# A fused embedding, attention and expert kernel: the split of the negated maxima moves to GpSimd, and the embedding steps run two at a time

## The chip, the core and the metric

The kernel runs on one core of one Trainium2 chip. The metric is the time of one execution on the device in microseconds, the median of three runs. The core has TensorE (PE, with PEld for its weight loads), VectorE (DVE), ScalarE (ACT), GpSimd (POOL) and SyncE (SP), which here only issues transfers. Each engine runs its own instructions in program order, and waits on semaphores for the others.

## What is computed

Eight batches of 1024 image tokens and 32 text tokens (1056 in all) with 64 features. The reference, cut to its body:

```python
h = _L0_tok_ref(x, L0_tok_W)                       # patches, real FFT, one linear map: (8, 1024, 64)
h = jnp.concatenate([h, txt], axis=1)              # (8, 1056, 64)
h = h + attn(_layernorm(h))                        # 4 heads of 16, softmax over all 1056 tokens, projection + bias
h = h + ffn(_layernorm(h))                         # top 2 of 8 experts, exact gelu, hidden width 128
```

The softmax of row n is exp(s - m) / sum exp(s - m), with m the largest score of the row. Everything is float32 in and out.

## The kernel before

**Two phases.** Phase 1 is attention for the eight batches, one *pass* each (passes 0 to 7), phase 2 the experts for four pairs of batches. Attention needs queries and keys to f32 precision, but multiplies in bf16: each value is split into three bf16 parts, and 96 rows of `q_stack` and `k_stack` hold the products of parts that matter. Three more rows of `q_stack` hold the negated row maximum, itself in three bf16 parts, against rows of ones in `k_stack`. So the score matmul delivers s - m, and ScalarE only takes the exponential.

**A pass and its units.** The queries stand in three chunks (384, 384 and 288 columns). A pass has 99 *units*, 33 per chunk: unit 0 of a chunk scores the 32 text keys, the other 32 score one tile of 128 keys for one head (L1185), and ScalarE exponentiates each (L927). The probabilities meet the values eight units later, four heads at a time in f32 (L1163), into one PSUM bank that ScalarE empties into `heads_out` (L912) six units into the next chunk. Scores rotate over three banks.

**Side work between the units.** Every engine runs the same generator, `run_phase1`. At each unit it does, in this order: `attend_unit`, `max_steps`, `weigh_unit` (L1163), `side_steps`. The tables `AT_...` give the unit of each side step:

- *Maxima.* For the next batch, 70 fills of PSUM per pass (25, 25 and 20 for the three chunks) recompute the scores without maximum (L1222, L1228, L1233), and VectorE reduces each (L1035, L1038, L1043). After the last of a chunk VectorE combines them into `negm` (L1049, and L1054 for the text queries), splits this in four small dependent steps into `neg_part` (L1058, L1060, L1063, L1065), and TensorE transposes that with an identity (the *shift*, L1244, L1248). VectorE copies the result to `m_part` (L1074) and SP sends it into `q_stack` with three DMAs (L790). The score of the chunk's first unit waits for these.
- *Where they stand.* `MAX_PLACE` spreads the 73 entries of `MAX_ORDER` over the units. The shift of a chunk follows two maxima of the next one: chunk 0 at unit 90 of the pass before its own, chunk 1 at unit 26, chunk 2 at unit 52 of the pass before. The last maximum of chunk 0 is at unit 85, of chunk 1 at 22, of chunk 2 at 48, and the first of the next batch at 49. Entries rotate over three banks by their index modulo 3; index 72 and the next index 0 share a bank. The very last shift stands at `LAST_SHIFT`, unit 49 of the last pass.
- *Tokenising* (passes 0, 2 and 4, for the pair of batches after next). Two halves of the image tokens are each built from eight embedding steps. A step is two f32 matmuls of 512 columns side by side in the two column halves of the array (L1199), in the trace four records, as f32 takes two passes. They stand at units 34, 36, ..., 48 and 50, 52, ..., 64, all in one side bank. ScalarE copies the first half to `h_new`, VectorE the second; norm, statistics and its square roots follow at 66 to 90.
- *Projecting* queries and keys at 36, 39, 42 (odd passes) or 92, 94, 97 (even): here GpSimd makes the third bf16 part (L856).
- *Finishing* the previous pass: reciprocals of the denominators on VectorE, their spread by DMA, the normalisation of the heads on GpSimd at units 24, 26, 28 (L862), and the output projection on TensorE at 27, 30, 33 (L1300), added to `h_res` by VectorE (L1104). Passes 1 to 7 have this.

In phase 1 GpSimd has nothing but L856 and L862. TensorE runs ahead of ScalarE by at most three units.

Of the kernel before, what the change touches and what calls it, by code (L numbers as in the profile page):

```python
# [8 lines left out]
ALU = mybir.AluOpType  # L9
# [16 lines left out]
NCH = 3  # L26
# [32 lines left out]
AT_FINISH = [27, 30, 33]  # L59
AT_SPREAD = [0, 2, 2]  # L60
AT_STACK = [1, 3]
AT_EMBED = [list(range(34, 49, 2)), list(range(50, 65, 2))]
AT_VARY = [74, 75, 76]
AT_ROOT = [77, 78, 79, 80]
AT_TOKENISE = [AT_EMBED[0][-1], AT_EMBED[1][-1], 66, 68, 70, 72, AT_VARY[-1], 86, 88, 90]
# [5 lines left out]
AT_LOAD = {"first": [2 + 3 * k for k in range(X_DMAS - X_EARLY)], "load": [30 + 3 * k for k in range(X_DMAS)]}  # L71
AT_FFN = 60

def max_order():

    order = [(0, 0, 0), (0, 0, 1), (-1, NCH - 1, None)] + [(0, 0, i) for i in range(2, MAX_OF[0])]
    for c in range(1, NCH):
        order += [(0, c, 0), (0, c, 1), (0, c - 1, None)] + [(0, c, i) for i in range(2, MAX_OF[c])]
    return order

# [44 lines left out]
def build(nc, x, txt, tok_w, w_qkv, w_proj, b_proj, gate_w, gate_b, w1, b1, w2, b2, consts, out):  # L126
    with ExitStack() as ctx:
# [3 lines left out]
        def sem(name):  # L131
            return ctx.enter_context(nc.semaphore(name))
# [77 lines left out]
        max_scores = sem("max_scores")  # L210
        max_done = sem("max_done")
        neg_max = sem("neg_max")
        neg_step = sem("neg_step")
        shifted = sem("shifted")
        scores_ready = sem("scores_ready")
# [81 lines left out]
        def side_steps(u, stages, b, par, q, g):  # L297

            ahead = q + 1 if par else q + 2
            order = []  # L300
            for i in range(3):
                if "finish" in stages and u == AT_SPREAD[i]:
                    order.append(("spread", i, b - 1, 1 - par, q, g))
            for i in range(2):
                if "following" in stages and u == AT_STACK[i] + (AT_FIRST["project"][-1] if "first" in stages else 0):
                    order.append(("stack", i, b + 1, 1 - par, q + 1, g))
            if u == AT_RECIP and "finish" in stages:
                order.append(("recip", 0, b - 1, 1 - par, q, g))
            if "load" in stages and u in AT_LOAD["load"]:
                order.append(("load", AT_LOAD["load"].index(u), None, None, q + 2, g))  # L310
            if "first" in stages and u in AT_LOAD["first"]:
                order.append(("load", X_EARLY + AT_LOAD["first"].index(u), None, None, 1, g))
            if "first" in stages and u == AT_FFN:
                order.append(("ffn", 0, None, None, None, g))
            for name, stage, at, t, tpar, pair in (
                    ("first", "project", AT_FIRST["project"], b + 1, 1 - par, q + 1),
                    ("first", "values", AT_FIRST["values"], b + 1, 1 - par, q + 1),
                    ("values", "values", AT_VALUES, b + 1, 1 - par, q + 1),
                    ("finish", "finish", AT_FINISH, b - 1, 1 - par, q),
                    ("tokenise", "tokenise", AT_TOKENISE, None, None, q + 2),  # L320
                    ("project", "project", AT_PROJECT["odd" if par else "even"], b + 2, par, ahead)):
                if name in stages:
                    if stage == "finish" and u in AT_NORMALISE:
                        order.append(("normalise", AT_NORMALISE.index(u), t, tpar, pair, g))
                    if stage == "tokenise" and u in AT_VARY[:-1]:
                        order.append(("vary", AT_VARY.index(u), None, None, pair, g))
                    if u in at:
                        order.append((stage, at.index(u), t, tpar, pair, g))
                    if stage == "tokenise":
                        for i in range(2):  # L330
                            if u in AT_EMBED[i][:-1]:
                                order.append(("embed", (i, AT_EMBED[i].index(u)), None, None, pair, g))
                        if u in AT_ROOT:
                            order.append(("root", 1 + AT_ROOT.index(u), None, None, pair, g))
                    g = g + USES[stage]
            return order
# [96 lines left out]
        def max_slot(t, c, i, n):  # L433

            if isinstance(t, int) and t == B - 1 and (c, i) == (NCH - 1, None):
                return MAXU * B - 1, 0, MAXU * B - 1
            t, n = (t + 1, n - MAXU) if n >= MAXU else (t, n)
            at = MAXU * t + n - 1
            if isinstance(t, int) and t == 0:
                at = n if n < 2 else n - 1  # L440
                return at, n % 3, at - 1 if n in (3, 4) else at - 2
            return at, n % 3, at if n == 0 else at - 2

        ROOT_STEPS = 16
# [291 lines left out]
        with nc.Block() as block:  # L736
# [112 lines left out]
            @block.gpsimd  # L849
            def _(pool):  # L850
                def side(stage, i, t, par, pair, g):
                    if stage == "project":

                        pool.wait_ge(part2_done, NCH * t + i + 1)
                        at_least(pool, stacked, 16 * 12 * t)
                        nc.gpsimd.tensor_tensor(qk_part[2][:, chunk[i]], qk_rest[:, chunk[i]], qk_part[1][:, chunk[i]],  # L856
                                                ALU.subtract).then_inc(part3_done, 1)
                    elif stage == "normalise":

                        pool.wait_ge(recip_spread, 16 * H * (t + 1))  # L860
                        pool.wait_ge(side_free, g)
                        nc.gpsimd.tensor_tensor(on[:, chunk[i]], ot[par][:, chunk[i]], recip[:, chunk[i]], ALU.mult)\  # L862
                          .then_inc(on_ready, 1)

                run_phase1(nc.gpsimd, lambda b, par, u, g: None, side, lambda b, par: None)

                def product(p, c, e):

                    n = PER_PAIR * p + E * c + e
                    dst = acc[p % 2][:, chunk[c]]  # L870
                    if (c, e) == (0, 0):
                        at_least(pool, out_full, FOLDS * (p - 1))
                    pool.wait_ge(y_read, n + 1)
                    if e > 0:
                        pool.wait_ge(summed, n)
                    nc.gpsimd.tensor_tensor(dst, h2_all[:, p, chunk[c]] if e == 0 else dst, prod[:, n % N_PROD, :],  # L876
                                            ALU.add).then_inc(summed, 1)

                run_phase2(nc.gpsimd, product, lambda eng, name, i, p: None, lambda p, i: None, side)

# [112 lines left out]
            def _(dve):  # L994
# [25 lines left out]
                def side(stage, i, t, par, pair, g):  # L1020
# [4 lines left out]
                    elif stage == "maxima":  # L1025
# [18 lines left out]
                              .then_inc(max_done, 1)  # L1044
                        if i == MAX_OF[c] - 1:
                            dve.wait_ge(max_done, at + 1)
                            step = 4 * (NCH * t + c)
                            kinds = slice(0, 1) if c < NCH - 1 else slice(1, 3)
                            last = nc.vector.tensor_reduce(negm[:, kinds.start, 0:nt, :], parts[:, 0:nt, :, :], AX.X,  # L1049
                                                           ALU.max, negate=True)  # L1050
                            if c == NCH - 1:
                                for h in range(H):
                                    rows = slice(32 * h, 32 * h + 32)
                                    last = nc.vector.tensor_reduce(negm[rows, 2, nt, h:h + 1], max_tail[rows, :],  # L1054
                                                                   AX.X, ALU.max, negate=True)
                            last.then_inc(neg_step, 1)
                            dve.wait_ge(neg_step, step + 1)
                            nc.vector.tensor_copy(neg_part[:, kinds, :, 0, :], negm[:, kinds, :, :]).then_inc(neg_step, 1)  # L1058
                            dve.wait_ge(neg_step, step + 2)
                            nc.vector.tensor_tensor(neg_rest[:, kinds, :, :], negm[:, kinds, :, :],  # L1060
                                                    neg_part[:, kinds, :, 0, :], ALU.subtract).then_inc(neg_step, 1)
                            dve.wait_ge(neg_step, step + 3)
                            nc.vector.tensor_copy(neg_part[:, kinds, :, 1, :], neg_rest[:, kinds, :, :]).then_inc(neg_step, 1)  # L1063
                            dve.wait_ge(neg_step, step + 4)
                            nc.vector.tensor_tensor(neg_part[:, kinds, :, 2, :], neg_rest[:, kinds, :, :],  # L1065
                                                    neg_part[:, kinds, :, 1, :], ALU.subtract).then_inc(neg_max, 1)
                    elif stage == "shift":

                        c = i[0]
# [335 lines left out]
```

## Time and profile before

| | |
|---|---|
| median of 3 runs | 876.16 us (873.74, 876.16, 883.76) |
| profiled execution | 872.1 us, its span 870.3 us |
| mean granted TensorE clock in it | 0.944 of full speed |
| prologue, to the first scores | to 89 us |
| attention, eight passes | 89 to about 683 us |
| experts | to the end |

The time of an execution includes a little beyond the span that the profile covers. In the rows, a line of a timeline has the start in us from the span's start, the length in us, the engine, the line of the kernel and what is written from what; in square brackets the engine's idle time just before and what ended it. Matmul records overlap: their lengths include a tail that the next one hides, so distances from start to start tell what an instruction costs. "POOLq" and the like are an engine's queue.

### The profile page before, as it was taken

How to read it: one execution, taken by the hardware profiler on the slowest of the kernel's cores; microseconds unless marked ns; L12 is line 12 of the kernel's file. 1: busy time of each engine (PE TensorE's matmuls, PEld its weight loads, DVE VectorE, ACT ScalarE, POOL GpSimd, SP SyncE). 2: the span in 40 equal slices, each digit the busy share in tenths (PEclk: the TensorE clock that was granted, in tenths of full speed). 3: DMA queues.
4: the chain of work that ended last, by engine and by line, in shares of the span. 5: the costliest groups of instructions: out<-in, count | busy, mean ns of one | idle time of the engine just before them, and what ended most of it. 6: DMA issues, size and time to landing. Idle time of an engine off the chain costs nothing.

```text
span 870.3 us, 14564 instructions
## 1 busy us (share of the span) xinstructions
PE 799.5 (92%) x5448; PEld 314.4 (36%) x5448; DVE 551.8 (63%) x1193; ACT 462.2 (53%) x1061; POOL 131.7 (15%) x148
## 2 busy tenths in 40 slices
PE   1958999999999989999999999999989899999995
PEld 1341322443332244333224433433334444545442
DVE  6038564678876467887656788788864075655632
ACT  1110454566664456666445666667655655464662
POOL 0010100012000001200000120010100055363664
PEclk9955699999999999999998999999988999999998
DMA  9329301016621001662100110220000736555571
GB/s 190 74 69 175 89 25 38 1 61 127 111 77 65 1 2 59 129 110 73 69 2 1 47 45 1 60 83 1 16 2 1 137 82 121 108 120 110 109 145 25
DMA packets 61934, 60.05 MB, mean 69 GB/s; under 512 B 23840, under 2 KB 54056, under 8 KB 61864
## 3 DMA queue, kind: packets, MB, share of 16 engines
q1 hardware_dynamic: 59264, 57.58, 30.2%
q10 hardware_dynamic: 2599, 1.54, 0.9%
q8 instruction: 43, 0.70, 0.3%
q14 instruction: 28, 0.22, 0.1%
HBM read 38.88 MB, written 2.57 MB: 48 GB/s over the span
## 4 chain that ended last, share of the span: by engine, by line
PE 78%; DVE 11%; ACT 4%; issue 2%; DMA 2%; POOL 0%; ACTq 0%; SPq 0%; POOLq 0%
PE bank L1163 15%; PE bank L1185 14%; PE bank L1222 11%; PE bank L1199 7%; PE bank L1331 7%; PE bank L1314 7%; DVE max_parts L1035 4%; PE bank L1276 3%; PE bank L1168 2%; PE bank L1300 2%; ACT probs L927 2%; PE bank L457 2%; PE bank L508 2%; PE bank L1280 1%; PE bank L633 1%
## 5 line engine op out<-in xcount | busy, mean ns | idle before, releaser
L1035 DVE TENSOR_REDUCE max_parts<-bank 128x1 f32<-128x512 f32 x512 | 331.3, 685 | 128.5 <-PE bank L1222 126.2
L927 ACT ACTIVATE probs<-bank 128x384 f32<-128x384 f32 (+1 forms) x768 | 311.6, 465 | 183.3 <-PE bank L1185 182.2
L1185 PE MATMUL bank<-q_stack,k_stack 99*128 99x384 bf16 (+1 forms) x768 | 227.6, 324 | 5.4 <-ACT probs L927 5.0
L1222 PE MATMUL bank<-k_stack,q_stack 96*128 96x512 bf16 x512 | 204.5, 402 | 6.3 <-DMA k_stack<-part 3.4
L1163 PE MATMUL bank<-probs,v_tiles 128*32 128x384 f32 (+1 forms) x1536 | 157.3, 482 | 2.2 <-ACT heads_out L912 2.1
L1185 PEld LDWEIGHTS bank<-q_stack,k_stack 99*128 99x128 bf16 x768 | 72.8, 100 | 199.9 <-ACT probs L927 151.7
L975 ACT ACTIVATE hid<-bank,biases 128x704 f32<-128x704 f32 x96 | 77.7, 844 | 58.9 <-PE bank L1331 58.6
L1123 DVE SCALAR_TENSOR_TENSOR prod<-bank,biases,cwb 128x352 f32<-128x352 f32 x96 | 55.3, 579 | 66.3 <-PE bank L1314 59.0
L876 POOL TENSOR_TENSOR acc<-acc,prod 128x352 f32<-128x352 f32 x84 | 78.2, 931 | 62.1 <-DVE prod L1123 58.1
L856 POOL TENSOR_TENSOR part<-qk_rest,part 128x352 bf16<-128x352 f32 x24 | 20.4, 851 | 365.8 <-DVE part L1083 365.8
L1314 PE MATMUL bank<-hid,w_sb 128*64 128x352 f32 x384 | 68.5, 476 | 1.5 <-DVE prod L1123 1.5
L1199 PE MATMUL bank<-x,tok_m 128*64 128x512 f32 x256 | 67.9, 628 | 1.7 <-DVE tok_m L1017 1.1
L1222 PEld LDWEIGHTS bank<-k_stack,q_stack 96*128 96x128 bf16 x512 | 50.6, 99 | 50.5 <-DVE max_parts L1035 24.2
L862 POOL TENSOR_TENSOR on<-heads_out,recip 128x352 f32<-128x352 f32 x24 | 21.9, 936 | 223.1 <-DMA recip<-recip_rows 223.1
L1163 PEld LDWEIGHTS bank<-probs,v_tiles 128*32 128x32 f32 x1536 | 30.7, 109 | 62.9 <-ACT probs L927 43.2
L1331 PE MATMUL bank<-xn,w_sb 64*128 64x352 f32 x192 | 36.4, 498 | 0.6 <-ACT hid L975 0.6
L1331 PE MATMUL bank<-xn_odd,w_sb 64*128 64x352 f32 x192 | 35.9, 491 | 0.6 <-ACT hid L975 0.6
L1314 PEld LDWEIGHTS bank<-hid,w_sb 128*64 128x64 f32 x384 | 23.5, 138 | 35.2 <-issue 28.3
L920 ACT ACTIVATE probs_tail<-bank 128x384 f32<-128x384 f32 (+1 forms) x24 | 11.1, 463 | 35.6 <-PE bank L1181 35.6
L936 ACT ACTIVATE part<-bank 128x352 bf16<-128x352 f32 x24 | 11.1, 464 | 30.5 <-PE bank L1276 30.4
L508 PE MATMUL bank<-ident_half,root_part 128*64 128x128 bf16 (+1 forms) x432 | 17.7, 228 | 8.5 <-DVE root_part L498 6.2
L1276 PE MATMUL bank<-xn,qkT 64*128 64x352 f32 x48 | 23.9, 592 | 1.2 <-DVE qk_rest L1080 0.6
(146 smaller groups left out, 579.2 us busy)
## 6 DMA issues: line engine op xcount, KB each, us to landing
cwb<-gates_by_expert SPq DMA_DIRECT2D x24, 704.0 KB, 11.3
x<-in_x SPq DMA_DIRECT2D x48, 256.0 KB, 7.0
q_stack<-part SPq DMA_DIRECT2D x48, 132.0 KB, 2.5
k_stack<-part SPq DMA_DIRECT2D x42, 132.0 KB, 2.4
x<-in_x SPq DMA_DIRECT2D x4, 576.0 KB, 12.0
h_res<-h_new SPq DMA_DIRECT2D x4, 528.0 KB, 3.0
recip<-recip_rows SPq DMA_DIRECT2D x32, 66.0 KB, 2.5
h_all<-h_res SPq DMA_DIRECT2D x4, 528.0 KB, 4.0
```

The costliest lines, as they stand in the source:

```text
L876: nc.gpsimd.tensor_tensor(dst, h2_all[:, p, chunk[c]] if e == 0 else dst, prod[:, n % N_PROD, :], ALU.add).then_inc(summed, 1)
L927: nc.scalar.activation(probs[:, group % 3, h, 0:n], src, ACT.Exp, scale=SCALE).then_inc(exp_done, 1)
L975: nc.scalar.activation(hid[:, n % N_HID, :, :], psum[:, first:first + 2, 0:CH], ACT.Gelu, bias=b1_sb[:, e:e + 1]).then_inc(gelu_done, 1)
L1035: nc.vector.tensor_reduce(max_parts[:, c, H * j + h, i % 2:i % 2 + 1], src[:, :], AX.X, ALU.max)\
L1123: nc.vector.scalar_tensor_tensor(out=prod[:, n % N_PROD, :], in0=banks[4 + n % 2][:, 0:CH], scalar=b2_sb[:, e:e + 1], in1=cwb[p % 2][:, e, ...
L1163: last = nc.tensor.matmul(o_bank[32 * h:32 * h + 32, 0:n], v_tiles[par][:, kt, h, :], probs[:, group % 3, h, 0:n], start=(kt == 0), stop=F ...
L1185: last = nc.tensor.matmul(bank[:, 0:n], ks[par][0:ROWS + 3, h, P * kt:P * kt + P], qs[par][0:ROWS + 3, h, QC[qc]], start=True, stop=True)
L1199: last = nc.tensor.matmul(bank[D * bp:D * bp + D, :], tok_m[:, part, :], xt[bp][:, first:first + NPATCH // 2, t4, :], start=(part == 0), s ...
L1222: last = nc.tensor.matmul(bank[:, :], queries(h, j), ks[par][0:ROWS, h, HALF * (i % 2):HALF * (i % 2) + HALF], start=True, stop=True)
L1276: last = nc.tensor.matmul(bank[:, 0:CH], qkT[rows, :], xn[rows, chunk[i]], start=True, stop=True)
L1314: last = nc.tensor.matmul(banks[4 + n % 2][D * bp:D * bp + D, 0:CH], w2_sb[:, m % E, :], hid[:, n % N_HID, bp, :], start=True, stop=True)
L1331: last = nc.tensor.matmul(banks[2 * (n % 2) + bp][:, 0:CH], w1_sb[rows, e, :], xn2[p % 2][rows, chunk[c]], start=True, stop=True)
```

## The change

- The four splitting steps leave VectorE and are issued by GpSimd, at the unit of the chunk's last maximum. VectorE signals a new semaphore, `neg_found`, after the reductions; GpSimd waits for it, and for its own previous step before each further one, and signals `neg_max` at the end.
- The shift stands behind three maxima of the next chunk instead of two: chunk 0 at unit 92, chunk 1 at 27, chunk 2 at 53; the third maximum takes its former place. `max_slot` is adapted. The last shift stays at 49.
- The embedding steps stand two at a time at units 34, 38, 42, 46 and 50, 54, 58, 62; the ones that end a half, and so the copies into `h_new`, at 46 and 62. Within a unit they come ahead of the other tokenising steps.

```diff
-AT_EMBED = [list(range(34, 49, 2)), list(range(50, 65, 2))]
+AT_EMBED = [[34, 34, 38, 38, 42, 42, 46, 46], [50, 50, 54, 54, 58, 58, 62, 62]]
...
+SHIFT_AFTER = 3
 def max_order():
-    order = [(0, 0, 0), (0, 0, 1), (-1, NCH - 1, None)] + [(0, 0, i) for i in range(2, MAX_OF[0])]
+    order = [(0, 0, i) for i in range(SHIFT_AFTER)] + [(-1, NCH - 1, None)] + [(0, 0, i) for i in range(SHIFT_AFTER, MAX_OF[0])]
     for c in range(1, NCH):
-        order += [(0, c, 0), (0, c, 1), (0, c - 1, None)] + [(0, c, i) for i in range(2, MAX_OF[c])]
+        order += [(0, c, i) for i in range(SHIFT_AFTER)] + [(0, c - 1, None)] + [(0, c, i) for i in range(SHIFT_AFTER, MAX_OF[c])]
...
+                    if stage == "tokenise":
+                        for i in range(2):
+                            for part, at_part in enumerate(AT_EMBED[i][:-1]):
+                                if u == at_part:
+                                    order.append(("embed", (i, part), None, None, pair, g))
...
-                at = n if n < 2 else n - 1
-                return at, n % 3, at - 1 if n in (3, 4) else at - 2
+                at = n if n < SHIFT_AFTER else n - 1
+                return at, n % 3, at - 1 if n in (SHIFT_AFTER + 1, SHIFT_AFTER + 2) else at - 2
...
# GpSimd, side():
+                    elif stage == "maxima" and i[1] == MAX_OF[i[0]] - 1:
+                        c = i[0]
+                        k = NCH * t + c
+                        kinds = slice(0, 1) if c < NCH - 1 else slice(1, 3)
+                        pool.wait_ge(neg_found, k + 1)
+                        nc.gpsimd.tensor_copy(neg_part[:, kinds, :, 0, :], negm[:, kinds, :, :]).then_inc(neg_step, 1)
+                        pool.wait_ge(neg_step, 3 * k + 1)
+                        nc.gpsimd.tensor_tensor(neg_rest[:, kinds, :, :], negm[:, kinds, :, :],
+                                                neg_part[:, kinds, :, 0, :], ALU.subtract).then_inc(neg_step, 1)
+                        pool.wait_ge(neg_step, 3 * k + 2)
+                        nc.gpsimd.tensor_copy(neg_part[:, kinds, :, 1, :], neg_rest[:, kinds, :, :]).then_inc(neg_step, 1)
+                        pool.wait_ge(neg_step, 3 * k + 3)
+                        nc.gpsimd.tensor_tensor(neg_part[:, kinds, :, 2, :], neg_rest[:, kinds, :, :],
+                                                neg_part[:, kinds, :, 1, :], ALU.subtract).then_inc(neg_max, 1)
...
# VectorE, side("maxima"), after the reductions:
-                            last.then_inc(neg_step, 1)
-                            dve.wait_ge(neg_step, step + 1)
...
+                            last.then_inc(neg_found, 1)
```

## Rows read from the trace of the kernel before

**Rows 1.** The page: TensorE's busy time; the last chain by engine.

```profile
PE 799.5 (92%) x5448; PEld 314.4 (36%) x5448; DVE 551.8 (63%) x1193; ACT 462.2 (53%) x1061; POOL 131.7 (15%) x148
...
PE 78%; DVE 11%; ACT 4%; issue 2%; DMA 2%; POOL 0%; ACTq 0%; SPq 0%; POOLq 0%
```

**Rows 2.** Two stretches: busy us of each engine, granted clock, DMA.

```profile
220.00:290.00 70.00, 68.64 (x486) 23.35 (x482) 50.49 (x100) 42.14 (x109) 2.72 (x3) 1.00 0.32 78
...
430.00:500.00 70.00, 68.51 (x478) 24.98 (x476) 43.00 (x97) 37.38 (x95) 2.56 (x3) 0.95 0.05 15
```

**Rows 3.** Timeline of TensorE, units 38 to 40: start us, length us.

```profile
276.02 0.38 PE L1222 MATMUL bank<-k_stack,q_stack 96*128 96x512 bf16 x1
276.33 1.08 PE L1199 MATMUL bank<-x,tok_m 128*64 128x512 f32 x4
277.34 0.34 PE L1185 MATMUL bank<-q_stack,k_stack 99*128 99x384 bf16 x1
277.52 0.38 PE L1222 MATMUL bank<-k_stack,q_stack 96*128 96x512 bf16 x1
277.74 0.33 PE L1185 MATMUL bank<-q_stack,k_stack 99*128 99x384 bf16 x1
277.99 1.08 PE L1199 MATMUL bank<-x,tok_m 128*64 128x512 f32 x4
```

**Rows 4.** Timeline of TensorE in the prologue: 28 embedding records in a row.

```profile
29.08 6.17 PE L1199 MATMUL bank<-x,tok_m 128*64 128x512 f32 x28
```

**Rows 5.** Timeline, shift of chunk 1, pass 1: VectorE, TensorE, GpSimd.

```profile
198.46 0.19 DVE L1049 TENSOR_REDUCE negm<-max_parts 128x12 f32<-128x36 f32 x1
...
199.29 0.17 DVE L1065 TENSOR_TENSOR neg_part<-neg_rest,neg_part 128x12 bf16<-128x12 f32 x1
...
199.61 0.23 PE L1244 MATMUL bank<-ident_half,neg_part 128*36 128x128 bf16 x1
199.77 0.34 PE L1185 MATMUL bank<-q_stack,k_stack 99*128 99x384 bf16 x1
...
200.44 0.81 PE L1300 MATMUL bank<-on,projT 128*64 128x352 f32 x2
...
196.01 2.70 POOL L862 TENSOR_TENSOR on<-heads_out,recip 128x352 f32<-128x352 f32 x3 [12.68 <-DMA recip<-recip_rows]
```

**Rows 6.** Timelines: dependent additions; start after VectorE; stretched subtraction.

```profile
857.02 4.14 POOL L876 TENSOR_TENSOR acc<-acc,prod 128x352 f32<-128x352 f32 x4 [0.72 <-DVE prod L1123]
...
216.06 0.34 DVE L1083 CAST part<-qk_rest 128x352 bf16<-128x352 f32 x1
...
216.48 0.85 POOL L856 TENSOR_TENSOR part<-qk_rest,part 128x352 bf16<-128x352 f32 x1 [1.29 <-DVE part L1083]
...
351.19 0.62 DVE L1060 TENSOR_TENSOR neg_rest<-negm,neg_part 128x12 f32<-128x12 f32 x1
```

**Rows 7.** Timeline of TensorE at the shift of chunk 0 in pass 1.

```profile
241.03 0.22 PE L1244 MATMUL bank<-ident_half,neg_part 128*36 128x128 bf16 x1 [0.16 <-DVE neg_part L1065]
```

**Rows 8.** Timeline of TensorE at units 48 and 49: passes 1, then 2.

```profile
218.29 0.34 PE L1185 MATMUL bank<-q_stack,k_stack 99*128 99x384 bf16 x1
219.08 0.38 PE L1222 MATMUL bank<-k_stack,q_stack 96*128 96x512 bf16 x1 [0.45 <-DVE max_tail L1043]
...
287.27 1.08 PE L1199 MATMUL bank<-x,tok_m 128*64 128x512 f32 x4
```

**Rows 9.** Timeline of TensorE at unit 41 of pass 6.

```profile
580.71 0.38 PE L1222 MATMUL bank<-k_stack,q_stack 96*128 96x512 bf16 x1
581.38 0.53 PE L1163 MATMUL bank<-probs,v_tiles 128*32 128x384 f32 x4 [0.29 <-ACT heads_out L912]
```

**Rows 10.** Timeline at the last shift: VectorE, then TensorE.

```profile
646.56 0.62 DVE L1054 TENSOR_REDUCE negm<-max_tail 32x1 f32<-32x3 f32 x4
...
648.18 0.26 PE L1244 MATMUL bank<-ident_half,neg_part 128*36 128x128 bf16 x1 [2.06 <-DVE neg_part L1065]
```

**Rows 11.** Timeline of TensorE at the first shift, in the prologue.

```profile
84.18 0.26 PE L1244 MATMUL bank<-ident_half,neg_part 128*36 128x128 bf16 x1 [0.98 <-DVE neg_part L1065]
```

More of the change, by code:

```diff
@@ L212, in build @@
         neg_max = sem("neg_max")
+        neg_found = sem("neg_found")
         neg_step = sem("neg_step")
@@ L329, in side_steps @@
                     if stage == "tokenise":
-                        for i in range(2):
-                            if u in AT_EMBED[i][:-1]:
-                                order.append(("embed", (i, AT_EMBED[i].index(u)), None, None, pair, g))
                         if u in AT_ROOT:
@@ L1046, in side @@
                             dve.wait_ge(max_done, at + 1)
-                            step = 4 * (NCH * t + c)
                             kinds = slice(0, 1) if c < NCH - 1 else slice(1, 3)
@@ L1055, in side @@
                                                                    AX.X, ALU.max, negate=True)
-                            last.then_inc(neg_step, 1)
-                            dve.wait_ge(neg_step, step + 1)
[L1058 to L1066, printed above, removed]
+                            last.then_inc(neg_found, 1)
                     elif stage == "shift":
```

## The prediction

> **What bounds the kernel now.** I read the page first. TensorE is busy 92% of the span and holds 78% of the chain that ended last, VectorE 11% and GpSimd nothing [rows 1]. The windows by stage come next: in attention TensorE is busy 68.5 of 70 us while VectorE has 43 to 51, ScalarE 37 to 42, GpSimd under 3 [rows 2]. So in attention only two things count: what the instructions in TensorE's own queue cost, and how long that queue stands at a wait. Work taken off VectorE is worth nothing unless TensorE waits for it. For both I read the timelines of TensorE unit by unit, comparing the distance from one start to the next for the same pair of lines.
>
> **Embedding steps in pairs.** One step is four records (two column halves at once, two passes). Alone between bf16 matmuls it holds TensorE from 276.33 to 277.34, 1.01 us. Also, a bf16 matmul of 512 columns before it takes 0.31 us to the next start (276.02 to 276.33) where before another bf16 matmul it takes 0.22 (277.52 to 277.74) [rows 3]. Together 1.10 us. In an unbroken run 28 records, seven steps, take 6.17 us; without the tail of the last record (0.6) that is 0.43 per pair of records, 0.86 per step [rows 4]. The rest, 0.24 us, is the price of each change of kind. Of 16 steps per tokenising pass eight no longer pay it. One of those (unit 36) stood right behind the weighted values, also f32, and paid only about 0.14. So 7 x 0.24 + 0.14 = 1.8 us per pass, in passes 0, 2 and 4: **-5.5 us**. The bounds are 0 (the second step of a pair loads weights as slowly as a lone one) and this; I take this, since the run of rows 4 is the same instructions back to back.
>
> **What the lone steps covered.** Moving steps to 34, 38, 42, 46 leaves units 40 and 48 without one. (a) Unit 48 holds the last maximum of chunk 2, unit 49 the first of the next pass, and by the numbering both use bank place 0. In pass 1, without embedding, TensorE goes from the scores at 218.29 to the maximum at 219.08, waiting for VectorE: 0.79 us where 0.17 is usual. In pass 2 the step at 287.27, one microsecond long, stands between and the wait is gone [rows 3, 8]. It comes back in three passes: 3 x 0.62 = **+1.9**. (b) Unit 41 multiplies the first probabilities of chunk 1 into the bank that ScalarE empties (L912) after unit 39. In pass 6, with no side work at 40, that costs 0.67 us after the maximum instead of 0.31 [rows 3, 9]. In tokenising passes the step at unit 40 (277.99) hides it; after the change the pair at 38 ends before the scores of unit 39, which release ScalarE, so it hides nothing: 3 x 0.36 = **+1.1**. The other moves (34, 50, the copies of h_new two units earlier) wait for nothing new: the pair at 34 still follows the same residual addition, and the loads of x are long done.
>
> **The split on GpSimd.** It is 24 chains (3 chunks, 8 passes) of four small dependent operations, two conversions and two subtractions of 12 or 24 elements; VectorE keeps the reductions. On VectorE each takes 0.17 us and the chain ends 0.81 us after the maxima are negated (198.65 to 199.46); TensorE starts the shift 0.15 later [rows 5]. The trace has no small operation on GpSimd. Bounds: VectorE's 0.17 below, and 0.93 above, its own operation over 352 elements [rows 6]. With 12 elements instead of 352 the lower end is nearer; I take 0.20 and call it x. Between dependent operations of GpSimd lie (4.14 - 0.93) / 3 - 0.93 = 0.14 us; from VectorE's end to GpSimd's start 0.08 (216.40 to 216.48) [rows 6]; from GpSimd to TensorE I take VectorE's 0.15. From the negated maxima to the shift: 0.08 + 4x + 3 x 0.14 + 0.15 = 1.45 us, where it was 0.96.
>
> **What queues behind that chain.** GpSimd runs in program order. The chain of chunk 1 stands at unit 22, the normalisations of the previous pass at 24, 26 and 28. Before, all three ran as soon as the reciprocals had landed, 196.01 to 198.71; the output projection at unit 27 (L1300, 200.44) needs the first [rows 5]. Now none can start before the maxima are negated (198.65) and split: 198.65 + 0.08 + 0.80 + 0.42 + 0.93 + 0.15 = 201.03. TensorE stands 0.59 us at L1300, in five of the seven passes with a projection. The shift in front of it, now at unit 27, is due 1.3 to 1.4 us after the negation and waits within that time. In passes 3 and 7 VectorE's own subtraction was stretched by the normalisations beside it (0.62 against 0.17) [rows 6], so the projection was late already: +0.14 and nothing. Together **+3.1**. The later normalisations (0.89 apart) stay ahead of units 30 and 33.
>
> **The other shifts.** Chunk 0, unit 90: TensorE waited about 0.2 us in four passes without tokenising [rows 7]; two units later it is due 1.8 us after the negation, and the wait goes: **-0.8**. Chunk 2 is due at 1.6 us, with 24 elements ready at 1.53: nothing. The last shift of all keeps its place, one unit behind the last maximum, where TensorE waits 2.06 us [rows 10]; the chain ends it: 1.01 us becomes 1.53, **+0.5**. In the prologue TensorE waits for the first split too [rows 11], but VectorE does a third maximum meanwhile (0.6), less than the 0.8 it no longer spends: the copy of m_part comes about 0.1 later there and once more in pass 0, **+0.2**. SP's three DMAs per shift keep their order except that one load of text now goes before those of chunk 0; they land over half a microsecond before the scores.
>
> **Sum.** -5.5 + 1.9 + 1.1 + 3.1 - 0.8 + 0.5 + 0.2 = **+0.5 us** on the profiled 872.1: 872.6. The median of the runs is 876.2, 4.1 higher, so 876.7. TensorE's granted clock, 0.95 in one stretch of pass 4 and 1.00 in another [rows 2], means half speed for some 7 of 70 us; such stretches may move or go with any change, worth up to 3 us. The likeliest case's own range is 873 to 881.
>
> **Rivals.**
> - *GpSimd's small operations are slow* (x = 0.4; slower). Seven projections wait 0.8 more (5.6), four shifts of chunk 0 0.4 each (1.7), four of chunk 2 0.65 (2.6), the last one 0.8, the prologue 1.6: +12.8, 889 by the median. It passes 1% at x = 0.35. For it: nothing small is measured. Against: 12 elements are few. Chance 0.20.
> - *A pair costs what two steps cost.* The 5.5 are missing: +6.0, 882.7. Rows 4 speak against. Chance 0.08.
> - *The waits do not come.* If GpSimd ends before L1300 (the negation comes earlier, x small) and units 41 and 49 find their banks free: -5.5 - 0.8 + 0.7 = -5.6, 870.6. For it: VectorE has less to do. Against: the negation follows the maximum of unit 22, which TensorE times. Chance 0.15.
> - *VectorE's relief carries* (faster). It loses 24 x 0.8 = 19 us, and holds 11% of the chain, 96 us [rows 1]. If a tenth of that goes, -9.5 with the rest at zero, 867. It decides if TensorE's waits for max banks were backlog; the ones I found follow TensorE's own last fill. Chance 0.10.
>
> **Chances.** The forecast has 0.47. One per cent, about what a measurement of this kernel can tell from no change, is 8.8 us. Faster comes from the relief and a little from the third rival with a better clock: 0.12. Slower is the slow GpSimd and part of the second with a worse clock: 0.24. Within 1%: 0.64. The range 868 to 889 leaves out the end of the fourth rival and the worst half of the first.
>
> **What would show it.** Right: eight records of L1199 in a row, 1.87 us to the next start; L1300 of unit 27 waiting for GpSimd's L862 by about 0.6 us; a start-to-start of 0.8 at unit 49 and 0.67 at 41 in tokenising passes; the four GpSimd operations at 0.2 us each. Wrong: those at 0.3 or more, or TensorE's waits for max_parts shrinking all over.

## The result, and the profile after

| | before | after |
|---|---|---|
| median, first measurement (18 executions each) | 880.85 us (869.0 to 891.6) | 867.11 us (860.9 to 871.7) |
| ratio of the two, 95% interval | | 0.990 (0.9875 to 0.993) |
| median, all executions with a granted clock on record (82 and 30) | 875.4 us | 868.4 us |
| mean of the same | 878.5 us | 867.8 us |
| lowest granted clock of an execution | 0.915 | 0.942 |
| profiled execution, its granted clock | 872.1 us, 0.944 | 870.6 us, 0.946 |

The change makes the kernel 1.0% faster in the first measurement and 0.5% in its repeat (e4 below: ratio 0.995, 0.992 to 0.999), and much steadier. The ratio leaves out slow executions, those that lie far above the fastest of their kernel; the medians and means here count all, because the spread turned out to be part of the effect. The first 18 executions of the kernel before (mean 881.3 us) have no granted clock on record and are not among the 82. The two profiled executions differ by 1.5 us only: 872.1 is under the median of before, 870.6 above that of after. Neither stands for its kernel's median, so the profile is read below by passes, and the time by many executions.

The page of the kernel after, its span, TensorE's busy time and the shares of the last chain:

```profile
span 868.8 us, 14564 instructions
...
PE 791.5 (91%) x5448; PEld 318.2 (37%) x5448; DVE 535.8 (62%) x1097; ACT 459.6 (53%) x1061; POOL 151.6 (17%) x244
...
PE 76%; DVE 10%; ACT 5%; issue 3%; DMA 2%; POOL 2%; ACTq 1%; SPq 0%; POOLq 0%
```

The chain is TensorE's as before [rows 1]; GpSimd now has 2% of it. Lengths of the passes, from the first scores of one pass to those of the next (chunk by chunk in brackets), from the timelines of L1181 before and L1190 after, where no clock change falls in:

| pass | before | after |
|---|---|---|
| 1 | 63.6 (22.3, 23.8, 17.6) | 63.7 (22.6, 23.7, 17.4) |
| 2, tokenising | 88.7 (22.3, 38.2, 28.2) | 87.4 (22.6, 37.4, 27.4) |
| 3 | 64.1 (22.7, 23.8, 17.6) | 63.7 (22.6, 23.7, 17.4) |

**GpSimd's small operations**, by the tile they write (count, then shortest, median and longest in ns):

```profile
L869 POOL CAST neg_part<-negm x24: 193/194/205, 82.8 to 645.0; 128x12 bf16<-128x12 f32 x16, 128x24 bf16<-128x24 f32 x8
L871 POOL TENSOR_TENSOR neg_rest<-negm,neg_part x24: 213/214/239, 83.1 to 645.3; 128x12 f32<-128x12 f32 x16, 128x24 f32<-128x24 f32 x8
L874 POOL CAST neg_part<-neg_rest x24: 194/195/204, 83.4 to 645.6; 128x12 bf16<-128x12 f32 x16, 128x24 bf16<-128x24 f32 x8
L876 POOL TENSOR_TENSOR neg_part<-neg_rest,neg_part x24: 213/214/241, 83.6 to 645.9; 128x12 bf16<-128x12 f32 x16, 128x24 bf16<-128x24 f32 x8
```

They take 0.19 and 0.21 us, the 0.20 that the sum was made with. The shift of chunk 1 in pass 1, VectorE, GpSimd, then TensorE:

```profile
200.61 0.19 DVE L1068 TENSOR_REDUCE negm<-max_parts 128x12 f32<-128x36 f32 x1
...
200.86 0.19 POOL L869 CAST neg_part<-negm 128x12 bf16<-128x12 f32 x1 [15.38 <-DVE negm L1068]
201.14 0.21 POOL L871 TENSOR_TENSOR neg_rest<-negm,neg_part 128x12 f32<-128x12 f32 x1
201.42 0.19 POOL L874 CAST neg_part<-neg_rest 128x12 bf16<-128x12 f32 x1
201.69 0.21 POOL L876 TENSOR_TENSOR neg_part<-neg_rest,neg_part 128x12 bf16<-128x12 f32 x1
201.86 2.70 POOL L882 TENSOR_TENSOR on<-heads_out,recip 128x352 f32<-128x352 f32 x3
...
202.14 0.23 PE L1253 MATMUL bank<-ident_half,neg_part 128*36 128x128 bf16 x1
202.93 0.78 PE L1309 MATMUL bank<-on,projT 128*64 128x352 f32 x2 [0.56 <-POOL on L882]
```

This answers to [rows 5]. The negation ends at 200.80; the split runs to 201.90 and the normalisations follow it in GpSimd's queue. L1309, the output projection of unit 27, waits 0.56 us for the first of them. It starts 2.13 us after the negation, before 1.79. The wait is 0.56 in all of passes 1 to 7, in 3 and 7 too.

**Pairs**: in pass 2 the weighted values of unit 41, then eight records in a row, then unit 49, which the lone step at 48 had covered (TensorE):

```profile
281.18 0.38 PE L1231 MATMUL bank<-k_stack,q_stack 96*128 96x512 bf16 x1
281.85 0.85 PE L1172 MATMUL bank<-probs,v_tiles 128*32 128x384 f32 x8 [0.29 <-ACT heads_out L932]
...
283.12 1.94 PE L1208 MATMUL bank<-x,tok_m 128*64 128x512 f32 x8
284.99 0.34 PE L1194 MATMUL bank<-q_stack,k_stack 99*128 99x384 bf16 x1
...
290.25 0.34 PE L1194 MATMUL bank<-q_stack,k_stack 99*128 99x384 bf16 x1
291.04 0.38 PE L1231 MATMUL bank<-k_stack,q_stack 96*128 96x512 bf16 x1 [0.46 <-DVE max_tail L1063]
```

A pair holds TensorE from 283.12 to 284.99, 1.87 us where two single steps held it 2 x 1.01; with the 0.09 that the bf16 matmul ahead of it takes longer, 1.96 where it was 2 x 1.10 [rows 3]. From the maximum at 281.18 to the weighted values it is 0.67 us, as in pass 6 before [rows 9], and from 290.25 to 291.04 it waits as pass 1 did before [rows 8].

**What I had not seen.** At unit 88 of each tokenising pass TensorE spreads the second third of the norm's roots (L508 before, L513 after) into the side bank, when VectorE has scaled xn from the first third. Before, VectorE's queue and then TensorE:

```profile
323.66 0.19 DVE L1049 TENSOR_REDUCE negm<-max_parts 128x12 f32<-128x36 f32 x1
323.88 0.17 DVE L1058 CAST neg_part<-negm 128x12 bf16<-128x12 f32 x1
324.08 0.17 DVE L1060 TENSOR_TENSOR neg_rest<-negm,neg_part 128x12 f32<-128x12 f32 x1
324.29 0.17 DVE L1063 CAST neg_part<-neg_rest 128x12 bf16<-128x12 f32 x1
324.49 0.17 DVE L1065 TENSOR_TENSOR neg_part<-neg_rest,neg_part 128x12 bf16<-128x12 f32 x1
324.57 0.55 DVE L1096 TENSOR_TENSOR xn<-xc,bank 128x384 f32<-128x384 f32 x1
...
325.18 0.52 PE L508 MATMUL bank<-ident_half,root_part 128*64 128x128 bf16 x12 [1.48 <-DVE xn L1096]
```

After, the same place:

```profile
325.31 0.19 DVE L1068 TENSOR_REDUCE negm<-max_parts 128x12 f32<-128x36 f32 x1
325.42 0.54 DVE L1105 TENSOR_TENSOR xn<-xc,bank 128x384 f32<-128x384 f32 x1
...
326.02 0.58 PE L513 MATMUL bank<-ident_half,root_part 128*64 128x128 bf16 x14 [0.65 <-DVE xn L1105]
```

VectorE's split of chunk 0 (L1058 to L1065) stood between the negation and the scaling (L1096, now L1105). With it on GpSimd the scaling follows at once, and TensorE's wait shrinks from 1.48 to 0.65 us. That is the 0.8 us of chunk 2 in the table. In the profile of before, passes 0 and 4 show less of it, as TensorE had come out of a stretch at half clock just ahead:

```profile
172.88 0.69 PE L508 MATMUL bank<-ident_half,root_part 128*64 128x128 bf16 x18 [0.48 <-DVE xn L1096]
...
479.22 0.69 PE L508 MATMUL bank<-ident_half,root_part 128*64 128x128 bf16 x18 [0.29 <-DVE xn L1096]
```

In e1, the same kernel profiled again, it is 1.47 us in all three passes.

The last shift of all waits a little longer, as forecast (2.06 in [rows 10]):

```profile
646.24 0.26 PE L1253 MATMUL bank<-ident_half,neg_part 128*36 128x128 bf16 x1 [2.37 <-POOL neg_part L876]
```

### The profile page after: what moved, and what is told of

The parts are those of the page before. It is cut to its first block, busy times and chain, and to the rows that moved or that the text cites. A ratio compares the mean times of both kernels' runs of the same rounds, so it can differ in the third digit from the quotient of the medians.

```text
span 868.8 us, 14564 instructions
## 1 busy us (share of the span) xinstructions
PE 791.5 (91%) x5448; PEld 318.2 (37%) x5448; DVE 535.8 (62%) x1097; ACT 459.6 (53%) x1061; POOL 151.6 (17%) x244
## 4 chain that ended last, share of the span: by engine, by line
PE 76%; DVE 10%; ACT 5%; issue 3%; DMA 2%; POOL 2%; ACTq 1%; SPq 0%; POOLq 0%
PE bank L1172 15%; PE bank L1194 13%; PE bank L1231 10%; PE bank L1208 7%; PE bank L1340 7%; PE bank L1323 7%; DVE max_parts L1055 4%; PE bank L1285 2%; PE bank L1177 2%; ACT probs L947 2%; PE bank L1309 2%; PE bank L462 2%; PE bank L513 2%; PE bank L1289 2%; DVE max_tail L1063 1%
## 5 line engine op out<-in xcount | busy, mean ns | idle before, releaser
L869 POOL CAST neg_part<-negm 128x12 bf16<-128x12 f32 (+1 forms) x24 | 4.7, 198 | 453.9 <-DVE negm L1068 345.5
L1208 PE MATMUL bank<-x,tok_m 128*64 128x512 f32 x256 | 63.3, 626 | 1.7 <-DVE tok_m L1037 1.1
L1172 PEld LDWEIGHTS bank<-probs,v_tiles 128*32 128x32 f32 x1536 | 30.8, 109 | 63.6 <-ACT probs L947 49.7
L1208 PEld LDWEIGHTS bank<-x,tok_m 128*64 128x64 f32 x256 | 16.9, 141 | 34.6 <-issue 33.4
L513 PE MATMUL bank<-ident_half,root_part 128*64 128x128 bf16 (+1 forms) x432 | 17.7, 228 | 8.0 <-DVE root_part L503 6.5
```

Of the source, the lines that this page charges most:

```text
L513: last = nc.tensor.matmul(bank[D * bp:D * bp + D, tokens.start - WIDE * i:tokens.stop - WIDE * i], root_part[0:n, part, col:col + 1].broad ...
L1172: last = nc.tensor.matmul(o_bank[32 * h:32 * h + 32, 0:n], v_tiles[par][:, kt, h, :], probs[:, group % 3, h, 0:n], start=(kt == 0), stop=F ...
L1208: last = nc.tensor.matmul(bank[D * bp:D * bp + D, :], tok_m[:, part, :], xt[bp][:, first:first + NPATCH // 2, t4, :], start=(part == 0), s ...
```

## The experiments

Each kernel ran 6 or 12 times beside the kernel before, e1 to e4 on one chip, e5 to e8 on a second, e9 to e12 on a third. Times scatter with the granted clock, and nearly on parallel lines: over the 196 executions of the twelve kernels one least-squares fit with an offset for each kernel and a common slope gives 7.3 us less per 0.01 of mean granted clock, with 1.5 us left over. So each kernel has two numbers: its time at an equal clock of 0.950 (what its instructions and waits cost; standard error 0.2 to 0.7 us), and how its clocks lie. The kernel before is at 872.1, 872.5 and 871.4 us on the three chips at equal clock, so times at equal clock compare across them to about half a microsecond. The share of its executions with a clock under 0.940 differs much more: 19 of 47, 3 of 17 and 8 of 18. Counts are therefore compared below with those of the kernel before on the same chip.

| kernel | n | at clock 0.950 | mean | mean clock | lowest clock | under 0.940 |
|---|---|---|---|---|---|---|
| before (e1 and the runs beside) | 82 | 872.0 | 878.5 | 0.941 | 0.915 | 30 |
| after (e4 and the first) | 30 | 866.8 | 867.8 | 0.949 | 0.942 | 0 |
| e2 pairs only | 12 | 869.7 | 872.0 | 0.947 | 0.933 | 3 |
| e3 split and shift only | 12 | 869.4 | 868.8 | 0.951 | 0.942 | 0 |
| e5 after, normalised early | 6 | 862.4 | 864.4 | 0.947 | 0.940 | 0 |
| e6 after, covered pairs | 6 | 863.7 | 862.6 | 0.952 | 0.947 | 0 |
| e7 chunk 0 on GpSimd only | 6 | 867.0 | 866.5 | 0.951 | 0.946 | 0 |
| e8 after, chunk 0 split twice | 12 | 870.3 | 872.6 | 0.947 | 0.941 | 0 |
| e9 before, scaling at 84 | 12 | 870.6 | 870.3 | 0.951 | 0.940 | 0 |
| e10 before, chunk 0 split twice | 6 | 874.9 | 887.6 | 0.933 | 0.914 | 3 |
| e11 after, both repairs | 6 | 859.1 | 860.2 | 0.949 | 0.944 | 0 |
| e12 both repairs, scaling at 84 | 6 | 859.2 | 859.2 | 0.950 | 0.944 | 0 |

**The kernel before, again** (no edit).

> The kernel before, unchanged, for its spread. Theory A (the instructions and waits of TensorE's queue explain the change): a second profile has the passes of 63.6 to 64.1 us (odd) and 88.7 (pass 2) again, ratio 1.000, and granted clocks scattered as the changed kernel's are (0.942 to 0.957). Theory B (the clock explains most of it): its mean granted clock lies lower than the changed kernel's in most executions, below 0.945, with half-clock stretches inside attention in the profile.

Ratio 1.0035 (0.9996 to 1.0074), odd passes 63.6 to 63.9, passes 2 and 4 at 88.7: theory A's part. But four of its twelve executions have a clock under 0.940, against none of 30 of the changed kernel: theory B's part. No execution under 0.940 was profiled (the lowest clock of a profile is 0.940, in e5), so where those lose their time is not shown. This profile, at 0.943, shows one place where time can go. TensorE's wait at unit 88 of pass 0, then windows of TensorE, PEld, VectorE, ScalarE and GpSimd busy time, granted clock, DMA:

```profile
177.13 0.69 PE L508 MATMUL bank<-ident_half,root_part 128*64 128x128 bf16 x18 [1.47 <-DVE xn L1096]
...
165.00:178.40 13.40, 11.50 (x128) 6.25 (x127) 9.99 (x35) 7.58 (x22) 0.00 (x0) 1.00 0.00 1
178.40:192.10 13.70, 13.70 (x70) 4.51 (x70) 6.37 (x14) 4.47 (x13) 2.56 (x3) 0.51 0.01 2
192.10:210.00 17.90, 17.34 (x135) 7.39 (x131) 13.71 (x27) 12.36 (x33) 2.72 (x3) 0.99 0.34 108
```

Right after the wait of 1.47 us the granted clock is half for 13.7 us; chunk 2 of pass 0 takes 33.8 us instead of 28.2 in the first profile. (All of pass 0 takes 103.9 instead of 94.1, but 4.3 of that is chunk 0, where the half clock of the prologue lasts longer.)

**One half at a time.**

```diff
# e2: before, with
-AT_EMBED = [list(range(34, 49, 2)), list(range(50, 65, 2))]
+AT_EMBED = [[34, 34, 38, 38, 42, 42, 46, 46], [50, 50, 54, 54, 58, 58, 62, 62]]
# e3: after, with the old AT_EMBED
```

> Only the embedding steps in pairs; split on VectorE and shift after two maxima as before. Theory A: chunk 1 of pass 2 (unit 33 to 66) is 0.86 us shorter than the 38.2 of before, the rest of the pass unchanged; three such passes give -2.6 us, ratio 0.997. Theory B: the pairs are what raises the clock; ratio 0.992, nearly the whole change, and no half-clock stretch inside tokenising passes.

> Only the split on GpSimd and the shift after three maxima; embedding steps single, at even units. Theory A: the projection at unit 27 starts 17.70 us after unit 0 as in the changed kernel (17.35 before), given back by unit 99; chunk 2 of tokenising passes is 0.76 us shorter; the last shift -0.2 to +0.3; in all -2 us, ratio 0.998. Theory B: if the clock comes from the split, ratio 0.992 here and 1.000 with the pairs only.

> The changed kernel, unchanged, beside the others on one chip. Both theories: ratio 0.990. Theory A says the sum of the two halves run alone gives it; theory B that its mean granted clock is higher by about 0.005 than that of the kernel before.

At equal clock the pairs give -2.3, the split and shift -2.6, together -4.9 of the -5.2 of the whole: the halves add. The ratios to the kernel before were 0.996 (0.992 to 1.000) for the pairs, 0.997 (0.993 to 1.001) for the split and 0.995 (0.992 to 0.999) for the whole change, again. For the whole change 0.990 was expected; 0.995 misses it, as the interval says, though the means of all executions on this chip are 9.7 us apart (878.8 and 869.1). In e2, chunk 1 of pass 4 is 37.5 us (before 38.2) and the wait at unit 88 is 1.47 us again in passes 0 and 4; in e3, chunk 2 is 27.4 (28.2), chunk 0 22.6 (22.3), as expected. The low clocks remain with the pairs (3 of 12) and are gone with the split (0 of 12, where the kernel before had 19 of 47 on this chip; so uneven a draw would come 5 times in 1000), so the steadiness comes from the split's side.

**The projection's wait.**

```diff
-AT_NORMALISE = [24, 26, 28]
+AT_NORMALISE = [19, 20, 21]
```

> The changed kernel with GpSimd's normalisations at units 19, 20 and 21 instead of 24, 26 and 28, so ahead of the split of chunk 1 in GpSimd's queue. Theory A (queue): the projection of unit 27 no longer waits 0.65 us, and starts 17.2 us after unit 0 instead of 17.70; at equal granted clock 2 to 3.5 us less than the changed kernel. Rival: the wait only moves to the shift or to ScalarE, and the pass stays at 63.67 us.

The normalisations of pass 1 run before the split in GpSimd's queue, and L1309 follows the shift without a wait (GpSimd, then TensorE):

```profile
198.18 2.71 POOL L882 TENSOR_TENSOR on<-heads_out,recip 128x352 f32<-128x352 f32 x3 [12.63 <-DMA recip<-recip_rows]
200.93 0.20 POOL L869 CAST neg_part<-negm 128x12 bf16<-128x12 f32 x1
...
202.28 0.76 PE L1309 MATMUL bank<-on,projT 128*64 128x352 f32 x2
```

At equal clock 4.4 us less than the changed kernel (+- 0.7), more than forecast; pass 1 takes 62.9 and pass 5 63.0 us instead of 63.7, pass 3 63.6. The first chunks of passes 1 to 7 together are 3.9 us shorter. Theory A holds; why pass 3 gains less is open.

**The cover of units 40 and 48.**

```diff
-AT_EMBED = [[34, 34, 38, 38, 42, 42, 46, 46], [50, 50, 54, 54, 58, 58, 62, 62]]
+AT_EMBED = [[36, 36, 40, 40, 44, 44, 48, 48], [52, 52, 56, 56, 60, 60, 64, 64]]
```

> The changed kernel with the pairs at units 36, 40, 44, 48 and 52, 56, 60, 64, so that units 40 and 48 have embedding work again. Theory A: the waits at unit 41 (0.36) and 49 (0.62) go in three passes, 2.9 us less than the changed kernel at equal clock, passes 2 and 4 at 86.4 us instead of 87.4. Rival: what follows each half is later by two units and costs it again; 0.

TensorE in pass 2, the pair at unit 48 and what follows:

```profile
287.39 1.94 PE L1208 MATMUL bank<-x,tok_m 128*64 128x512 f32 x8
289.26 0.34 PE L1194 MATMUL bank<-q_stack,k_stack 99*128 99x384 bf16 x1
289.43 0.38 PE L1231 MATMUL bank<-k_stack,q_stack 96*128 96x512 bf16 x1
289.74 0.85 PE L1172 MATMUL bank<-probs,v_tiles 128*32 128x384 f32 x8
```

From the scores of unit 49 to its maximum it is 0.17 us now, where the changed kernel has 0.79. Passes 2 and 4 take 86.1 us, 1.3 less each, where the two waits account for 0.97; at equal clock -3.1, expected -2.9.

**Which split matters.** Only chunk 0 goes to GpSimd, single steps, shift after three maxima:

```diff
-                    elif stage == "maxima" and i[1] == MAX_OF[i[0]] - 1:
+                    elif stage == "maxima" and i[0] == 0 and i[1] == MAX_OF[i[0]] - 1:
# and VectorE keeps its four steps for c > 0
```

> Single embedding steps; shift after three maxima; only the split of chunk 0 on GpSimd, those of chunks 1 and 2 on VectorE as before. Theory C: VectorE's split of chunk 0 stands in front of its scaling of xn at unit 86, for which TensorE waits 1.48 us at L508; taking it away is most of what the split alone gave (-2.5 us at equal clock) and is what keeps the clock up, so no execution has a granted clock below 0.940. Theory A without C: the clock's low executions come back, as two thirds of the splits are where they were.

A third of the splits on GpSimd does more than all of them: 867.0 at equal clock, against 869.4 for e3, since the projection does not wait for GpSimd. Chunk 0 takes 22.0 us, against 22.3 before: there the shift of chunk 1 at unit 27 instead of 26, with the third maximum ahead of it, is all that differs, so the later shift is itself worth 0.26 us. The wait at unit 88 is 0.65 in passes 0 and 4. No execution is under 0.946, but with 3 of 17 for the kernel before on this chip six executions cannot tell.

**VectorE made late again.** In e8, after VectorE's negation of chunk 0, its four old steps run once more into unused tiles:

```diff
                             last.then_inc(neg_found, 1)
+                            if c == 0:
+                                ... # the same two casts and two subtractions, negm -> again_part
```

> The changed kernel with the four splitting steps of chunk 0 done on VectorE once more, into tiles that nobody reads, so that VectorE is as late at unit 86 as before while all else stays. Theory C: TensorE's wait at L508 is 1.5 us again, 2.5 us more than the changed kernel at equal clock, and executions with a granted clock under 0.940 return (about one in three). Rival (the clock follows something else, such as the pairs or the order of the shift): 2.5 us more, and no execution under 0.940.

3.5 us more than the changed kernel at equal clock, expected 2.5, and the wait is back at 1.49 (passes 0 and 4). For the clock the expectation failed: no execution is under 0.940, which is what its rival said. It does not decide for the rival either, as the kernel before had only 3 of 17 on this chip, and by that rate none of twelve would come one time in ten. Two executions are at 0.941, and the profiled execution is one of these, with the longest half-clock stretch seen within the passes, again right behind the wait (TensorE, then windows):

```profile
477.36 0.69 PE L516 MATMUL bank<-ident_half,root_part 128*64 128x128 bf16 x18 [1.49 <-DVE xn L1120]
...
465.00:478.40 13.40, 11.48 (x127) 6.45 (x128) 9.99 (x34) 7.54 (x22) 0.81 (x4) 1.00 0.01 1
478.40:505.70 27.30, 27.30 (x126) 11.21 (x125) 12.38 (x23) 10.49 (x28) 2.55 (x3) 0.50 0.10 31
505.70:530.00 24.30, 23.75 (x152) 7.73 (x150) 18.50 (x33) 15.24 (x37) 4.32 (x8) 1.00 0.16 47
```

27.3 us at half clock, over units of pass 4 and pass 5 that take 11.0 us longer than in passes 2 and 3 (34.5 for 28.3 and 27.4 for 22.6).

**The cause without GpSimd.** One number of the kernel before:

```diff
-AT_TOKENISE = [AT_EMBED[0][-1], AT_EMBED[1][-1], 66, 68, 70, 72, AT_VARY[-1], 86, 88, 90]
+AT_TOKENISE = [AT_EMBED[0][-1], AT_EMBED[1][-1], 66, 68, 70, 72, AT_VARY[-1], 84, 88, 90]
```

> The kernel before with one number changed: the first third of the norm is spread and scaled at unit 84 instead of 86, so ahead of the last maximum and the split of chunk 0 in VectorE's queue. Nothing is on GpSimd, no pair, no later shift. Theory C (TensorE's wait of 1.5 us at L508 of unit 88 is what lets the clock fall for long): that wait is under 0.7 us, 1 to 2.5 us less than before at equal clock, no half-clock stretch over 7 us, and the executions under a granted clock of 0.940, a third of those of before, are gone. Rival (the split's place, or GpSimd's activity, matters in another way): executions under 0.940 stay at a third.

```profile
477.06 0.69 PE L508 MATMUL bank<-ident_half,root_part 128*64 128x128 bf16 x18 [1.27 <-DVE root_part L498]
```

The wait at unit 88 is gone, but a wait for the roots takes its place at unit 84, 1.27 us long; my expectation of under 0.7 was wrong. Still chunk 2 is 27.5 us, 0.7 shorter, the time at equal clock 1.4 less (0.7 +- 0.6 against the kernel before on the same chip), and no execution is under 0.940 (one is at 0.940). The kernel before had 8 of 18 beside it; so uneven a draw would come 7 times in 1000.

**More of the cause.**

```diff
# the kernel before, chunk 0 split twice on VectorE
```

> The kernel before with the split of chunk 0 done a second time on VectorE, into tiles that nobody reads: the wait at L508 grows from 1.5 to 2.3 us. Theory C: 2.5 us more at equal clock, and executions under 0.940 become the rule, over half. Rival: 2.5 us more, share of a third unchanged.

The wait is 2.16 us in pass 0, and only 3.4 us at half clock follow it (TensorE, then a window; in passes 2 and 4, behind other half-clock stretches, it is 1.20 and 1.19):

```profile
177.40 0.97 PE L511 MATMUL bank<-ident_half,root_part 128*64 128x128 bf16 x18 [2.16 <-DVE xn L1110]
...
177.70:181.10 3.40, 3.40 (x36) 1.46 (x33) 1.68 (x4) 0.82 (x2) 0.00 (x0) 0.50 0.00 0
```

At equal clock 2.9 us more, the mean 887.6. Ratio 1.011 (1.003 to 1.020). Three of six executions are under 0.940, two of them at 0.917 and 0.914; the kernel before had 8 of 18 beside it, down to 0.919, so a larger share is not shown.

**Both repairs.**

> The changed kernel with both repairs: normalisations at units 19, 20, 21 and pairs at 36, 40, 44, 48, 52, 56, 60, 64. Theory A: the gains add, -4.4 and -3.1 at equal clock, 859.3 us at 0.950; pass 2 takes 85.3 us, odd passes 62.95.

> The kernel of both repairs, and the first scaling at unit 84 as well. Theory A: of the remaining wait of 0.65 us at L508 about half goes in three passes, 1 us less, 858 us at 0.950. Rival: at unit 84 the roots are not ready (VectorE ends them half a microsecond later), so the wait only moves forward; 0.

e11 is at 859.1 for equal clock, where 859.3 was expected; pass 2 takes 85.5 us, pass 1 62.9. Its ratio to the kernel before is 0.987 (0.982 to 0.992), its mean 18 us lower, 7.6 us under the changed kernel's. The earlier scaling adds nothing at equal clock (859.2): the rival was right, the wait for the roots comes forward (1.27 us in pass 4).

## Why the prediction was wrong

It forecast no change (+0.5 us, range 868 to 889); measured was -1.0%, 867.1. Step by step:

- *What bounds the kernel*: right. TensorE's queue was the place to read.
- *Pairs, -5.5, and the two uncovered waits, +1.9 and +1.1*: right, for a pass -0.84 in sum; chunk 1 is -0.86 in the changed kernel (pass 2) and -0.75 with the pairs alone (e2, pass 4). The waits at 41 and 49 appeared where forecast, and e6 took them away.
- *GpSimd's operations at 0.20*: right. The rival of slow small operations is refuted, by 0.19 and 0.21 us on GpSimd against 0.17 on VectorE.
- *The projection's wait, +3.1*: right in place and releaser, too large in size. Between dependent steps lies 0.08 us, not the 0.14 of the long additions, so it came 2.13 instead of 2.38 us after the negation. By unit 33 passes 1, 2, 4, 5 and 6 are 0.3 longer, pass 3 0.1 shorter and pass 7 0.25 shorter: some +1.2, and that contains the 0.26 per pass which the later shift gives back (e7) and for which the prediction had no term.
- *The other shifts*: chunk 2 of passes 1, 3, 5 and 6 is 0.16 shorter each (forecast 0.2), the last shift +0.3 (forecast +0.5). Chunk 1 of the same four passes is 0.10 shorter, which no term had. The prologue's first scores start at 87.7 to 90.0 us in the profiles of all kernels, too much scatter to read 0.1 from.
- *What failed: "Work taken off VectorE is worth nothing unless TensorE waits for it", and then the waits I looked for.* I measured waits as the excess of one pair of lines over the same pair elsewhere. Within passes 1 to 6 L508 stands only in the tokenising ones, so no other pass could give the excess, and the wait at unit 88 looked like the price of L508; the three tokenising passes themselves differed, with 0.48, 1.48 and 0.29 us. The timeline's bracket names it in plain words, 1.48 us for VectorE's xn. The forecast put the way of VectorE's relief into L508 at nothing; measured is 0.76 in chunk 2 of each tokenising pass at full clock, -2.3 us in all. The fourth rival (VectorE's relief carries, -9.5 us, chance 0.10) had this direction, but neither the place nor the size.
- *What failed: the clock, put at nothing in the sum and, as something that "may move or go with any change", at up to 3 us in the range*. The mean granted clock rises from 0.941 to 0.949, worth 0.0075 x 732 = 5.5 us of the mean. With -5.2 at equal clock this makes the 10.7 us between the means. From the single profile of before, at 872.1 under the kernel's median of 875.4, I could not have read the spread; the three times given, 873.7 to 883.8, already showed that there was one.

By passes the traces give 3 x -0.86, +1.2, 3 x -0.76, 4 x -0.16, 4 x -0.10 and +0.3, together -4.4; at equal clock the measurement says -5.2 +- 0.4. Somewhat under a microsecond is not placed. Of the distance between the forecast's +0.5 and these -4.4, 2.3 is the wait at unit 88, 1.9 the projection that was put too high, and the rest small terms.

**What is shown and what stays open.** Shown: VectorE's split of chunk 0, ahead of the scaling of xn, costs 0.8 us in each tokenising pass. Shown too: with the split on GpSimd the executions under 0.940 are gone (e3 and e4, 0 of 24, against 19 of 47 for the kernel before on that chip), and with the pairs alone they are not. That the wait at unit 88 is what brings them is argued, not shown. For it: e9 shortens that stretch without GpSimd, and has none under 0.940 against 8 of 18. And in the fourteen profiles two half-clock stretches that begin within passes 0 to 6 are longer than 7 us (the one from the prologue into pass 0, which every profile has, aside); both began within 1.3 us of the end of a wait of 1.47 to 1.49 us at that place, and none followed a wait of 0.65. Against it, or undecided: waits of 1.47 also passed without a stretch (passes 2 and 4 of e1, 0 and 4 of e2), the wait of 2.16 in e10 was followed by 3.4 us only, e9 keeps a wait of 1.27 without low clocks, e8 has the wait back and no execution under 0.940, and e10, with a longer wait, has no larger share of them than the kernel before beside it. The mean clock also moves elsewhere: in the profiles the half-clock time of the prologue varies from 55 to 68 us, and that behind pass 6 from 14 to 29 us. So half of the 10.7 us between the means comes with the split through the clock, by a way that stays open.

## What to carry to other kernels

Before calling work on a side engine free, follow its queue to the next thing that the bounding engine waits for, and take each wait from the idle time and releaser that the timeline states: a wait at a line that stands only in some passes hides from a comparison with the others. When work moves to an idle engine, look at what already queues there and let the older work go first; here an order of three numbers was worth 4.4 us. And where executions of one kernel spread by 3%, compare at an equal granted clock, look separately at what makes the clock low, and count low clocks only against the kernel before on the same chip: its share ran from 3 of 17 to 19 of 47.

## What the hardware showed that I had not expected

A wait of TensorE of a microsecond and a half in the midst of dense work was twice followed by a long stretch at half clock: 13.7 us in e1, which made the chunk 5.6 us longer, and 27.3 us in e8, which made the same units 11.0 us longer. In most cases nothing followed, and that the wait was the cause is not shown. Small operations on GpSimd (12 or 24 elements per partition) take 0.19 to 0.21 us, with 0.08 us between dependent ones, hardly more than VectorE's 0.17.
